# A graph kernel: kept edges copied to fixed places by ScalarE, and message steps of VectorE without register loads

## What is computed

```
# block 1: mean of edge features by source
sums = segment_sum(edge_attr, src);  counts = segment_sum(1, src)
edge_attr_agg = sums / max(counts, 1)
# block 3: degree-normalised messages (MSG)
norm = deg_inv_sqrt[src] * deg_inv_sqrt[dst]
out = segment_sum(h[src] * norm[:, None], dst)
```

## Time and profile before

| | us |
|---|---|
| median of 3 runs (3276.77 to 3283.07) | 3277.62 |
| the profiled execution, its own time | 3274.19 |
| its span | 3272.4 |
| PE / DVE / ACT / POOL busy | 2268.7 / 2012.1 / 880.7 / 2037.9 |
| mean granted TensorE clock, as a share of full | 0.825 |

### The profile page before, as it was taken

How to read it: one execution, slowest core, us unless ns; L and a number is a source line. 1 busy time by engine, 2 the same in 40 slices (tenths; PEclk the granted TensorE clock), 3 DMA queues, 4 the chain that set the end, 5 groups by cost and what they waited for, 6 DMA issues and landing times.

```text
span 3272.4 us, 49254 instructions
## 1 busy us (share of the span) xinstructions
PE 2268.7 (69%) x14349; PEld 2076.5 (63%) x14350; DVE 2012.1 (61%) x3304; ACT 880.7 (27%) x2321; POOL 2037.9 (62%) x1707
## 2 busy tenths in 40 slices
PE   0000177789999667996778763777887765698997
PEld 0000066678888667776778753666666655598997
DVE  8789897433333212664666657865665563588887
ACT  0000022200000000334444422344444422254544
POOL 5777877777777771012444435567777721287886
PEclk9999998855555555998999986899998985699999
DMA  6543355554444341220111114567777733322231
GB/s 204 150 116 85 87 147 154 151 160 113 117 113 117 85 106 63 76 69 27 43 42 47 45 64 128 142 166 189 190 195 193 191 90 112 77 63 78 63 86 35
DMA packets 341516, 358.58 MB, mean 110 GB/s; under 512 B 209280, under 2 KB 248560, under 8 KB 341125
## 3 DMA queue, kind: packets, MB, share of 16 engines
q1 hardware_dynamic: 209538, 196.84, 20.5%
q0 software_dynamic: 105984, 93.52, 12.6%
q10 hardware_dynamic: 25853, 66.46, 6.6%
HBM read 234.90 MB, written 122.85 MB: 109 GB/s over the span
## 4 chain that ended last, share of the span: by engine, by line
POOL 32%; PE 26%; issue 16%; DVE 13%; DMA 7%; DVEq 3%; ACT 2%; another core or an unknown queue 0%; SPq 0%; POOLq 0%; ACTq 0%
POOL sorted L996 27%; PE ps L2139 4%; DMA x_rows<-mid 3%; PE ps L2158 3%; PE ps L2039 3%; PE ps L2149 3%; DVEq L1605 2%; POOL h_lo L1035 2%; DVE hT L1615 2%; PE ps L1990 2%; DVE yb L1880 2%; PE ps L2017 2%; PE ps L2094 1%; PE ps L2096 1%; PE ps L2095 1%
## 5 line engine op out<-in xcount | busy, mean ns | idle before, releaser
L1990 PE MATMUL ps<-big 128*128 128x65 f32 x2380 | 528.5, 419 | 116.4 <-DVE big L1371 64.4
L1073 POOL DMA_INDIRECT mid<-h_rows,idx_a x400 | 484.7, 1212 | 181.9 <-issue 113.1
L1990 PEld LDWEIGHTS ps<-big 128*128 128x128 f32 x2380 | 514.0, 331 | 132.1 <-issue 131.3
L1005 POOL TENSOR_TENSOR rstd<-var,neg_half 125x2 f32<-125x2 f32 (+1 forms) x100 | 71.5, 715 | 452.6 <-DVE var L1422 452.6
L1370 DVE COPY mid<-big 128x28 f32 (+1 forms) x85 | 21.4, 252 | 476.3 <-PE ps L1990 282.6
L996 POOL DMA_INDIRECT sorted<-yb,idx_a x200 | 239.3, 1197 | 84.0 <-issue 60.3
L996 POOL DMA_INDIRECT sorted<-wk,idx_a x200 | 237.6, 1188 | 61.0 <-issue 61.0
L996 POOL DMA_INDIRECT sorted<-mid,idx_b x200 | 237.4, 1187 | 61.0 <-issue 60.7
L996 POOL DMA_INDIRECT sorted<-xh,idx_b x200 | 237.3, 1187 | 61.0 <-issue 61.0
L2158 PE MATMUL ps<-adj,h_in_r 128*128 128x304 f32 (+3 forms) x980 | 238.5, 369 | 44.1 <-issue 40.1
L1615 DVE TENSOR_TENSOR hT<-ps,mid 128x608 bf16<-128x608 f32 (+3 forms) x245 | 254.8, 1040 | 0.1
(11 more groups left out here) (331 smaller groups left out, 6599.6 us busy)
## 6 DMA issues: line engine op xcount, KB each, us to landing
h_in_r<-h_parts SPq DMA_DIRECT2D x245, 256.0 KB
big<-sorted ACTq DMA_DIRECT2D x85, 469.0 KB
sorted<-hT SPq DMA_DIRECT2D x73, 469.0 KB
mid<-in_L_ffn_w SPq DMA_DIRECT2D x16, 1024.0 KB
hid_x<-hT ACTq DMA_DIRECT2D x25, 500.0 KB
mid<-hid_x SPq DMA_DIRECT2D x25, 500.0 KB
h_parts<-h_part_r SPq DMA_DIRECT2D x25, 500.0 KB
mid<-h_rows,idx_a POOLq DMA_INDIRECT x400
```

Of the source, the lines that this page charges most:

```text
L1005: nc.gpsimd.tensor_tensor(out_, in_, neg_half[:, 0:in_.shape[1]], ALU.pow).then_inc(done, 1)
L1073: nc.gpsimd.indirect_dma_start(mg4[:, s, i, :], None, h_rows, bass.IndirectOffsetOnAxis(idx4[:, s, i:i + 1], 0)).then_inc(s_gk[s], 16)
L1990: i_ = mm(banks[:, bass.ds(o_, CW)], node_hot[:, s % 2, i, :], rows2[:, s, i, 0:CW], start=False, stop=True, skip_group_check=True)
```

## The change

Four parts. (1) ScalarE gets 20 short loops, `place_kept(c, part)`, one behind `low_column(b)` at 20 of the blocks 50 to 72 (`KEEP_AT`, 13, 12, 12 and 12 buckets a loop). Each of the 245 iterations loads a word of `first_words` and copies the 2 or 3 tiles of a bucket from `keep` to a fixed place in `kept`. The words are now set on VectorE during the positions. Each loop first waits until VectorE has copied the first group behind the chunk (`s_keep`). (2) SyncE writes `kept` (539 columns) instead of `keep` (647) and waits for the 20 loops instead of the bucket means. VectorE copies 48 of the 85 groups to `keep`. (3) Six VectorE operations ahead of the message steps compute all `dst_rel` at once. (4) `select_edges` has no register loads, no L1607 and one `node_sel` operation.

```diff
-            sp.wait_ge(s_a0, 1)
-            sp.dma_start(sorted_ends, keep[:, :, 0:KD]).then_inc(s_endk, 16)
+            sp.wait_ge(s_kset, ND * len(KEEP_PARTS))
+            sp.dma_start(sorted_ends, kept).then_inc(s_endk, 16)
...
+            def place_kept(c, part):
...
+                act.wait_ge(s_keep, sum(CG[:c + 1]) + 1)
+                with act.Fori(*KEEP_PARTS[part]) as h:
+                    first = act.value_load(first_words[0:1, bass.ds(c * TB + h, 1)], min_val=0, max_val=KD - CAPS[c])
...
+                    act.activation(to[:, :, bass.ds(h, 1), o_:o_ + CAPS[c]].rearrange("p c a k -> p c (a k)"), keep[:, :, bass.ds(first, CAPS[c])], ACT.Copy)
+                act.nop(nofuse=True).then_inc(s_kset, 1)
...
             for b in blocks:
                 low_column(b)
+                for c in range(ND):
+                    if 0 <= b - KEEP_AT[c] < len(KEEP_PARTS):
+                        place_kept(c, b - KEEP_AT[c])
...
+                    v.tensor_scalar(first_words[:, c * TB:(c + 1) * TB], ps[0:1, 4, 128:128 + TB], float(GFIRST[c] * GA), None, ALU.add).then_inc(s_dve, st.up())
...
             def select_edges(r, h, q, i):
...
-                for c in chunks:
-                    first = dve.value_load(first_words[0:1, bass.ds(c * TB + h, 1)], min_val=0, max_val=KD - CAPS[c])
...
-                    v.tensor_tensor(dst_rel[:, s, o_:o_ + CAPS[c]], kept_dst[:, bass.ds(first, CAPS[c])],
-                                    to_rel[MADD.index((r, c))][:, bass.ds(h, 1), :].rearrange("p a t -> p (a t)"), ALU.add).then_inc(s_rel, 1)
...
-                for o_, first, k in firsts:
-                    v.tensor_tensor(node_sel[:, s, o_:o_ + k, :], near[:, 0:BR].unsqueeze(1).to_broadcast([BR, k, BR]),
-                                    kept_lo[:, bass.ds(first, k)].unsqueeze(2).to_broadcast([BR, k, BR]), ALU.is_equal)
-                dve.wait_ge(s_rel, REL + RELS[r] + (q - r * TB + 1) * len(chunks) + 12 * len(chunks) * i)
+                v.tensor_tensor(node_sel[:, s, 0:n, :], near[:, 0:BR].unsqueeze(1).to_broadcast([BR, n, BR]),
+                                kept_lo[:, bass.ds(h * n + KEPT_AT[r], n)].unsqueeze(2).to_broadcast([BR, n, BR]), ALU.is_equal)
                 v.tensor_tensor(dst_sel[:, s, 0:n * w].rearrange("p (k w) -> p k w", w=w), near[:, 0:w].unsqueeze(1).to_broadcast([BR, n, w]),
-                                dst_rel[:, s, 0:n].unsqueeze(2).to_broadcast([BR, n, w]), ALU.is_equal).then_inc(s_dsel2, 1)
+                                dst_rel[:, bass.ds(h * n + REL_AT[r], n)].unsqueeze(2).to_broadcast([BR, n, w]), ALU.is_equal).then_inc(s_dsel2, 1)
...
-                v.tensor_copy(first_words, tab_in[0:1, ND * TB:2 * ND * TB]).then_inc(s_tabs, sorted_.up())
...
+                    v.tensor_tensor(dst_rel[:, REL_AT[r]:REL_AT[r] + TB * n].rearrange("p (h k) -> p h k", h=TB)[:, :, o_:o_ + CAPS[c]],
+                                    kept_dst[:, KEPT_AT[r]:KEPT_AT[r] + TB * n].rearrange("p (h k) -> p h k", h=TB)[:, :, o_:o_ + CAPS[c]],
+                                    to_rel[k], ALU.add).then_inc(s_tabs, sorted_.up())
```

More of the change, by code:

```diff
@@ L35 @@
 FIRST_OF = (0, 0, 2, 3, 4)
-KT = GA * sum(CG)
+NK = 48
 KD = GA * sum(CG[:ND]) + max(CAPS)
+STEP_TILES = tuple(sum(CAPS[c] for c in chunks) for _, chunks, _ in RANGES)
+KEPT_AT = tuple(TB * sum(STEP_TILES[:r]) for r in range(len(RANGES) - 1)) + (TB * sum(STEP_TILES[:len(RANGES) - 2]),)
+REL_AT = tuple(TB * sum(STEP_TILES[:r]) for r in range(len(RANGES)))
+KS = TB * sum(STEP_TILES[:-1])
+KEEP_AT = (50, 56, 60, 65, 69)
+KEEP_PARTS = ((0, 13), (13, 25), (25, 37), (37, 49))
+assert GA * NK >= KD
 FARM = 131072.0
@@ L42 @@
 NB = NODES + 128
+FIRST_OF_RANGE = tuple(min(r for r in range(len(RANGES)) if c in RANGES[r][1]) for c in range(ND))
 MADD = tuple((r, c) for r in range(len(RANGES)) for c in RANGES[r][1])
@@ L137, in build @@
         tab_kept = dram("tab_kept", BR, 2 * ND * TB + ND)
-        sorted_ends = nc.dram_tensor("sorted_ends", (BR, 2, KD), f32, kind="Internal").ap()
+        sorted_ends = nc.dram_tensor("sorted_ends", (BR, 2, KS), f32, kind="Internal").ap()
         x3_rows = dram("x3_rows", NODES, XW)
@@ L247, in build @@
         btab = big[:, 11200:11200 + 2 * ND * TB + ND]
+        first_words = big[0:1, 11700:11700 + ND * TB].bitcast(i32)
         assert o <= 2 * 8 * N
@@ L270, in build @@
         agg = mid[0:BR, 0:TB * DE].rearrange("p (t d) -> p t d", t=TB)
-        keep = mid[0:BR, 3200:3200 + 2 * KT].rearrange("p (c t) -> p c t", c=2)
+        keep, o = cut(mid, BR, 3200, 2 * GA * NK)
+        keep = keep.rearrange("p (c t) -> p c t", c=2)
+        kept, o = cut(mid, BR, o, 2 * KS)
+        kept = kept.rearrange("p (c t) -> p c t", c=2)
+        assert o <= 5850
         wA1e = mid[0:DE, 5850:5850 + HID0]
@@ L387, in build @@
         s_const = sem("constants_set")
+        s_keep, s_kset = sem("sorted_ends_copied"), sem("sorted_ends_placed")
         s_rawT = sem("ends_transposed")
@@ L428, in build @@
         s_radd, RADD = s_x0, G
-        s_rel, REL = s_csel, G
         s_accT, ACCT = s_cmm, G
@@ L709, in load_sorted @@
                 act.dma_start(rows2[:, s], sorted_v[c][:, j * GA:(j + 1) * GA, :]).then_inc(s_srow[s], 16)
+            def place_kept(c, part):
+                r = FIRST_OF_RANGE[c]
+                o_ = sum(CAPS[k] for k in RANGES[r][1] if k < c)
+                to = kept[:, :, KEPT_AT[r]:KEPT_AT[r] + TB * STEP_TILES[r]].rearrange("p c (h k) -> p c h k", h=TB)
+                act.wait_ge(s_keep, sum(CG[:c + 1]) + 1)
+                with act.Fori(*KEEP_PARTS[part]) as h:
+                    first = act.value_load(first_words[0:1, bass.ds(c * TB + h, 1)], min_val=0, max_val=KD - CAPS[c])
+                    first = nc.s_assert_within(first, 0, KD - CAPS[c], skip_runtime_bounds_check_because="a bucket starts at a tile of its chunk")
+                    act.activation(to[:, :, bass.ds(h, 1), o_:o_ + CAPS[c]].rearrange("p c a k -> p c (a k)"), keep[:, :, bass.ds(first, CAPS[c])], ACT.Copy)
+                act.nop(nofuse=True).then_inc(s_kset, 1)
             groups = list(range(NGA))
@@ L1362, in _, with sorted_hot @@
             v.tensor_scalar(deg[:, :], cnt[:, :], 1.0, None, ALU.max).then_inc(s_deg, 1)
-            def sorted_hot(g, s=None):
+            def sorted_hot(g, s=None, kept=True):
                 s = g % NS if s is None else s
@@ L1369, in sorted_hot, with sorted_hot_late @@
                     dve.wait_ge(s_a2, g - 1)
-                v.tensor_copy(keep[:, :, bass.ds(g * GA, GA)], rows2[:, s, :, CW:RW].rearrange("p t c -> p c t"))
+                if kept:
+                    v.tensor_copy(keep[:, :, bass.ds(g * GA, GA)], rows2[:, s, :, CW:RW].rearrange("p t c -> p c t")).then_inc(s_keep, 1)
                 v.tensor_tensor(node_hot[:, s % 2], lo_near.unsqueeze(1).to_broadcast([BR, GA, BR]),
                                 rows2[:, s, :, CW:CW + 1].to_broadcast([BR, GA, BR]), ALU.is_equal).then_inc(s_hot2, 1)
-            in_turns(dve, Steps(), sorted_hot, NGA, NS, NGA % NS, NS)
+            def sorted_hot_late(g, s=None):
+                sorted_hot(g, s, kept=False)
+            in_turns(dve, Steps(), sorted_hot, NK, NS, 0, NS)
+            in_turns(dve, Steps(), sorted_hot_late, NGA, 0, NGA % NS, NS, first=NK)
             dve.wait_ge(s_a2, NGA)
```

22 lines of the change are left out of this document (9 added, 13 removed).

## The result

| | us | ratio to the kernel before | 95% interval |
|---|---|---|---|
| before, beside the first measurement, median of 6 | 3280.35 | | |
| the changed kernel, first measurement, median of 6 (3251.72 to 3264.82) | 3257.28 | 0.9932 | 0.9917 to 0.9946 |
| the same program, second measurement, median of 5 (3229.40 to 3245.33) | 3237.87 | 0.9879 | 0.9861 to 0.9896 |
| the same program, third measurement, median of 4 (3236.33 to 3246.55) | 3240.18 | 0.9893 | 0.9877 to 0.9910 |

The account below looks back on a forecast made before the run. The prediction took VectorE's steps to limit the first of five message ranges and GpSimd the other four. It summed 36.6 + 1 - 0 = 37.6 us won, forecasting a median of 3240 us, range 3231 to 3272 us.

Parts of the forecast that it names:

- Message stage: First range's steps on VectorE get shorter, so GpSimd sets the pace there: 36.6 us won, 25 to 40 us possible.
- The 16 turns: First message range, half block 3 to 19: 7.6 us a turn, 121.6 us instead of 157.8, 36.2 us won.
- the start: Beginning of the message steps: the first waiting gather comes at 2009.4 instead of 2011.85 us, 2.4 us won.
- the 2 us given back at the ranges' ends: Message stage: VectorE waits for TensorE's products at each range's end, now with GpSimd lacking spare time; 2 us deducted.
- Reading back: Reading `sorted_ends` back, 9.38 us in the chain: fewer table columns save 1 us (0 to 1.6).
- Bucket stage: ScalarE's new loops, at 1.2 us an iteration, stay hidden behind TensorE's pace: cost 0, up to 55 us at 1.51.
- the formula: Bucket-stage cost: 20 x (loop + 1.5 - 17.1) - 9 us, for 20 blocks, TensorE's 17.1 us a block and 9 us lead.
- At 1.2 us I put it at 0: Bucket stage: at 1.2 us an iteration, a loop of 15.1 us stays under the 15.6 us limit and costs nothing.
- The sign for being wrong that the prediction named: Bucket stage: GpSimd's L996 waiting for ScalarE's L651 in 950 to 1130 us; separately, ScalarE loads of 0.45 us or more.
- The rival that the prediction set beside it: Bucket stage: slow ScalarE loads starve GpSimd, costing 37 to 55 us; chance 0.06 of cancelling the gain, 0.08 of slower.
- The ring of VectorE and TensorE: First message range: the two engines keep waiting for each other, 8.2 us a turn, 9.6 us less won, 3250 us; chance 0.14.
- In part: Bucket stage: GpSimd starves partly at 1.34 us an iteration, loop 16.8 us, cost 15 us, 3255 us; chance 0.10.

Follow-up runs that it names:

- the last measurement: Two kernels with the loops written out, against the kernel before: with four gathers of five per half block, 3153.51 us (0.9629); otherwise unedited, 3239.02 us (0.9888).
- four edits: Against the changed kernel, each loop made one copy, 3234.20 us; halved with a load behind each half, 3240.67; spread over more blocks, 3239.35; written out, 3232.91.

## Why the prediction was right, step by step

**Message stage: right.** Forecast 36.6 us. In the second and third measurement, first gather to last, it was 610.4 and 610.3 us, 40.6 less than before (in the first, 38.2). The 16 turns took 121.2 us (forecast 121.6); the start won 3.0 us (2.4); the 2 us given back at the ranges' ends weren't lost, and the few waits of the later ranges, 1 us, went too, as the upper bound had it. `node_sel` takes 0.81 us (0.80), the step 2.30 (2.27), VectorE's turn 7.16 (7.05), `dst_rel`'s set-up 1.23 (1.4). The clock granted in the first range is 0.95 in the second measurement, 0.89 in the first (above 0.9 was said). No run takes the parts of the VectorE edit one by one, so what the register loads, the sums set ahead and the single `node_sel` are each worth is the prediction's account and isn't shown.

**Reading back: off, and small.** 9.19 us in the first profile and 9.13 in the second against 9.38: 0.2 us, not 1. With 539 columns instead of 647, a sixth less, it took 2 to 3% less time, so it doesn't go in proportion to its columns.

**Bucket stage: right in its structure, too dear in an iteration, and blind to one thing.** The load is 0.279 us (0.27 forecast), the iteration 1.07 (1.2). The runs with two and three loads bear the formula out: nothing is lost at a loop of 15.4 us and 121 us at 22.0, so the threshold lies between them; that it is at 15.6 us follows from the formula's slope and wasn't measured by itself. (For 1.51 us an iteration the formula gives 57 us, not the 55 that the prediction has.) The step that failed in the first measurement is "At 1.2 us I put it at 0", which rests on "TensorE's pace still sets ScalarE's" with a pace of 6.84 us a group. There a group took 7.5, and the formula takes this pace as given. The sign for being wrong that the prediction named, puts waiting for ScalarE between 950 and 1130 us, came; the reason that it named, loads of 0.45 us or more, didn't.

The Trainium skill's page DMA: Bandwidth & Descriptors (Latency and other measured facts) has a floor of some 600 ns for such a load. These runs contradict it: 0.272 at least and 0.279 us at the median of 245 in the second measurement. The rival that the prediction set beside it, in which GpSimd starves behind a ScalarE that is too slow, is real, as three loads show; with one load the kernel stays clear of it.

**Rivals.** The ring of VectorE and TensorE at 8.2 us a turn is out: 7.58, and 7.16 where GpSimd lets it. "In part" (3255 us) named the first measurement's size and place, by a wrong cause.

**Sum.** 36.6 + 1 + 0 were forecast and 40.6 + 0.2 + 0 came in the traces, 3240 us against 3238 and 3240; the first measurement lost 20.7 us of it in the bucket stage. That the later medians come within 2 us of the forecast is in part luck: the message stage won 4 us more than forecast, and single executions of one measurement lie up to 16 us apart (3229 to 3245). That the first measurement lies inside the range owes as much to the range's width, for the prediction had no term for a disturbed pace.

**What stays open** is what makes the pauses. On ScalarE's and TensorE's queues they are in 3 of the 14 profiles (the first, and weakly in the two of the last measurement), always between 750 and 1135 us, when ScalarE loads registers one behind another; the profile of the kernel before and that without the loops have none there, but nine with such loads have none either. In the same three profiles and in that of the kernel before, and in no other, SyncE's queue has them between 2000 and 2600 us. So they go with the occasion and not with the change; the change puts work where they cost something. They don't go with the chip alone either: the third measurement and the last one ran on one chip, the former without them. And that they cost the 20.7 us is argued, from one disturbed profile and from what the other runs leave: no run brings them about. That the first measurement's other executions, which carry no profile, were slow for the same reason is inferred from their times.

## What to carry to other kernels

When a work item is put on an idle engine's queue, count its time against the period of what that queue feeds, here a block's 17.1 us: below it costs nothing, beyond it each microsecond counts in every period. Leave room below, since the period of the other engines can be longer at times as well (7.5 us a group here instead of 6.8). And before a loss is explained, measure the unedited kernel again beside the first experiment: four edits here seemed to remove what wasn't in the program.

## What the runs showed of the hardware

- A loop iteration on ScalarE with a register load, a bound, a computed address and one small copy takes 1.04 us undisturbed; written out, 0.64 (0.69 on average); each further load of a word with its bound adds 0.54 to 0.57 us. The copy of 4 to 6 columns (0.21 us) lies beside it.
- The same program can lose 18 us of 3240 in one measurement and not in two others, with the granted clock (0.823, 0.821, 0.824) and the kernel before unchanged.
- An instruction's minimum and maximum in one line are a quick test for such pauses: 18/18/29 ns undisturbed, 3/18/515 disturbed, at one median. They can stand in a queue where they cost nothing, as in SyncE's of the kernel before (3/33/216).
- GpSimd's indirect DMAs follow each other every 1.491 us in some profiles and 1.494 in others, of one program too: 2 us over 800 of them, to be taken off before a difference of that size is read as an effect.
